# A causal attention between two expert layers: the order of work within a step

## What is computed

```python
S = where(mask, q @ k.T, 0)                # q, k with rotary positions
wk = exp(sk); zk = cumsum(wk, axis=time)   # sk, sv: clipped slot logits
p = softmax((S @ wk) * scale / zk)
wv = exp(sv); zv = cumsum(wv, axis=time)
A = where(mask, (p / zv) @ wv.T, 0)
o = A @ v
o = o * rsqrt(mean(o * o) + EPS) * gnorm_w * g * sigmoid(g)
x = x + o @ Wo
```

## Time and profile before

| | us |
|---|---|
| median of 3 runs | 529.92 (529.62 to 530.06) |
| the profiled execution | 530.72 |
| its span, first to last instruction | 528.8 |
| attention, from the first `project` to the last `add_y` | 193.5 to 368.0 |

### The profile page before, as it was taken

How to read it: one execution, slowest core, us unless ns; L and a number is a source line. 1 busy time by engine, 2 the same in 40 slices (tenths; PEclk the granted TensorE clock), 3 DMA queues, 4 the chain that set the end, 5 groups by cost and what they waited for, 6 DMA issues and landing times.

```text
span 528.8 us, 12332 instructions
## 1 busy us (share of the span) xinstructions
PE 467.3 (88%) x3895; PEld 318.7 (60%) x3895; DVE 427.0 (81%) x1139; ACT 309.1 (58%) x667; POOL 173.3 (33%) x198
## 2 busy tenths in 40 slices
PE   1788999999999568998898999885889999999996
PEld 0344566666665556676776776764455666666664
DVE  3598999999999835777778777866599999999997
ACT  3543555555555675877777777653555555555553
POOL 2999960000000364566566666534000000000000
PEclk9998999999999785999999999996599999999999
DMA  6212000000000000000000000000000000000002
GB/s 204 90 61 78 1 0 0 0 0 0 0 1 1 1 1 0 2 1 2 0 0 0 0 0 0 0 1 0 2 1 2 0 0 0 0 0 0 0 0 79
DMA packets 6697, 6.98 MB, mean 13 GB/s; under 512 B 818, under 2 KB 5170, under 8 KB 6676
## 3 DMA queue, kind: packets, MB, share of 16 engines
q1 hardware_dynamic: 6532, 6.33, 3.9%
q10 hardware_dynamic: 144, 0.39, 0.2%
HBM read 5.67 MB, written 1.05 MB: 13 GB/s over the span
## 4 chain that ended last, share of the span: by engine, by line
PE 60%; DVE 19%; issue 9%; ACT 7%; POOL 2%; DVEq 1%; DMA 1%; POOLq 0%; ACTq 0%
PE bank L1128 15%; PE bank L1140 10%; PE bank L1141 10%; PE bank L1142 10%; DVE h L804 4%; PE bank L1311 3%; DVE h_lo L810 2%; ACT gate_s L313 2%; PE bank L1325 2%; PE bank L1275 2%; DVE stats L702 2%; DVE pz L934 1%; DVE x L793 1%; DVE logit_c L926 1%; PE bank L1230 1%
## 5 line engine op out<-in xcount | busy, mean ns | idle before, releaser
L318 ACT ACTIVATE h_hi<-h 128x512 f16<-128x512 f32 x144 | 90.7, 630 | 133.3 <-DVE h L804 133.3
L804 DVE SCALAR_TENSOR_TENSOR h<-bank,gate_s 128x512 f32<-128x512 f32 x144 | 99.4, 690 | 28.4 <-ACT gate_s L313 19.0
L1128 PE MATMUL bank<-w_hi,h_hi 128*128 (+1 forms) x576 | 106.4, 221 | 12.9 <-DVE h_lo L810 8.3
L1140 PE MATMUL bank<-xt_hi,w_hi 128*128 128x512 f16 x288 | 111.8, 388 | 0.0
L1141 PE MATMUL bank<-xt_hi,w_lo 128*128 128x512 f16 x288 | 111.7, 388 | 0.0
L1142 PE MATMUL bank<-xt_lo,w_hi 128*128 128x512 f16 x288 | 111.5, 387 | 0.0
L1128 PE MATMUL bank<-w_hi,h_lo 128*128 (+1 forms) x576 | 105.9, 221 | 0.0
L1128 PE MATMUL bank<-w_lo,h_hi 128*128 (+1 forms) x576 | 105.9, 221 | 0.0
L810 DVE TENSOR_TENSOR h_lo<-h,h_hi 128x512 f16<-128x512 f32 x144 | 100.6, 698 | 0.1
L793 DVE SCALAR_TENSOR_TENSOR x<-bank,wts,x 128x128 f32<-128x128 f32 x288 | 86.5, 343 | 1.6 <-PE bank L1128 1.1
L313 ACT ACTIVATE gate_s<-bank 128x512 f32<-128x512 f32 x144 | 83.5, 580 | 0.6 <-PE bank L1142 0.6
(11 more groups left out here) (159 smaller groups left out, 855.7 us busy)
## 6 DMA issues: line engine op xcount, KB each, us to landing
wf<-in_w_ffn SPq DMA_DIRECT2D x8, 384.0 KB, 3.1
x<-in_x SPq DMA_DIRECT2D x4, 256.0 KB, 4.9
out_dram<-x SPq DMA_DIRECT2D x4, 256.0 KB, 2.3
cst<-in_consts SPq DMA_DIRECT2D x1, 455.0 KB, 5.3
wf<-in_w_ffn ACTq DMA_DIRECT2D x1, 384.0 KB, 4.2
wqkvg<-in_w_qkvg SPq DMA_DIRECT2D x1, 256.0 KB
wslots<-in_w_slots SPq DMA_DIRECT2D x3, 64.0 KB
wo<-in_w_out SPq DMA_DIRECT2D x1, 64.0 KB
```

Of the source, the lines that this page charges most:

```text
L318: act.activation(h_hi[:, g, ih, :], h32[:, ih, :], ACT.Copy).then_inc(hhi_done, 1)
L804: nc.vector.scalar_tensor_tensor(h32[:, ih, :], up_ps[ih][:, :], HS / (XS * WS), gate_s[:, ih, :], ALU.mult, ALU.mult).then_inc(hmul_done, 1)
L1128: i = mm(dst, hp[:, g, ih, c * P:(c + 1) * P], wcols(wp, e, at, D), start=(k == 0), stop=(k == 3 * IH - 1))
L1140: mm(ps[:, :], wcols(w_hi, e, at, P), xt_hi[:, ts], start=True, stop=False)
```

## The change

The lists of all four engines are put in another order. The functions, the stages, the semaphores, the buffers and the count of instructions are the same.

```diff
--- before.py
+++ after.py
@@ -458,23 +458,23 @@
                 if mid:
                     sums_log(*mid)
                 if mid:
-                    copy_value_slots(*mid)
-                if mid:
                     sums_first_inverse(*mid)
+                if front:
+                    qk_high(*front)
                 if end:
                     copy_o(*end)
                 if front:
-                    qk_high(*front)
-                if front:
                     slots_high(*front)
                 if front:
                     slots_exponent(*front)
+                if mid:
+                    copy_value_slots(*mid)
                 if front:
                     copy_qk_parts(*front)
+                if mid:
+                    soft_exp(*mid)
                 if front:
                     slots_middle(*front)
-                if mid:
-                    soft_exp(*mid)
                 if last:
                     o_square(*last)
                 if front:
@@ -655,10 +655,10 @@
                     qk_low(*front)
                 if front:
                     slots_rest(*front)
-                if front:
-                    slots_low(*front)
                 if last:
                     gate_o(*last)
+                if front:
+                    slots_low(*front)
                 if last:
                     root_o(*last)
 
@@ -1000,10 +1000,10 @@
                 front, mid, last, end = stages(i, n)
                 if front:
                     rope_multiply(*front)
+                if front:
+                    clip_slots(*front)
                 if end:
                     norm_apply(*end)
-                if front:
-                    clip_slots(*front)
                 if last:
                     mask_a(*last)
                 if last:
@@ -1012,22 +1012,22 @@
                     sums_product(*mid)
                 if mid:
                     sums_inverse(*mid)
+                if mid:
+                    soft_scale(*mid)
+                if mid:
+                    soft_min(*mid)
+                if mid:
+                    soft_centre(*mid)
+                if last:
+                    norm_shares(*last)
+                if mid:
+                    prob_scale(*mid)
+                if mid:
+                    prob_total(*mid)
+                if last:
+                    norm_squares(*last)
                 if end:
                     add_y(*end)
-                if mid:
-                    soft_scale(*mid)
-                if mid:
-                    soft_min(*mid)
-                if last:
-                    norm_shares(*last)
-                if mid:
-                    soft_centre(*mid)
-                if mid:
-                    prob_scale(*mid)
-                if last:
-                    norm_squares(*last)
-                if mid:
-                    prob_total(*mid)
                 if last:
                     norm_variance(*last)
                 if mid:
@@ -1341,34 +1341,34 @@
                 front, mid, last, end = stages(i, n)
                 if front:
                     project(*front)
+                if front:
+                    slot_logits(*front)
                 if mid:
                     running_sums(*mid)
+                if last:
+                    weights_a(*last)
                 if mid:
                     turn_v(*mid)
-                if front:
-                    slot_logits(*front)
                 if end:
                     turn_o(*end)
-                if last:
-                    weights_a(*last)
                 if mid:
                     logits_of_earlier(*mid)
+                if mid:
+                    logits_of_chunk(*mid)
                 if end:
                     out_proj(*end)
-                if mid:
-                    logits_of_chunk(*mid)
                 if front:
                     turn_qk(*front)
                 if last:
                     outputs(*last)
                 if mid:
+                    add_sums(*mid)
+                if mid:
                     add_state(*mid)
                 if mid:
-                    add_sums(*mid)
+                    turn_p(*mid)
                 if front:
                     scores(*front)
-                if mid:
-                    turn_p(*mid)
 
             pe.wait_ge(consts_loaded, 16)
             turn(0, 0)
```

More of the change, by code:

```diff
@@ L657, in attn_step @@
                     slots_rest(*front)
+                if last:
+                    gate_o(*last)
                 if front:
                     slots_low(*front)
-                if last:
-                    gate_o(*last)
                 if last:
@@ L1014, in attn_step @@
                     sums_inverse(*mid)
-                if end:
-                    add_y(*end)
                 if mid:
@@ L1023, in attn_step @@
                 if mid:
-                    soft_centre(*mid)
+                    prob_scale(*mid)
                 if mid:
-                    prob_scale(*mid)
+                    prob_total(*mid)
                 if last:
                     norm_squares(*last)
-                if mid:
-                    prob_total(*mid)
+                if end:
+                    add_y(*end)
                 if last:
@@ L1343, in attn_step @@
                     project(*front)
+                if front:
+                    slot_logits(*front)
                 if mid:
                     running_sums(*mid)
-                if mid:
-                    turn_v(*mid)
-                if front:
-                    slot_logits(*front)
-                if end:
-                    turn_o(*end)
                 if last:
@@ L1354, in attn_step @@
                 if mid:
+                    turn_v(*mid)
+                if end:
+                    turn_o(*end)
+                if mid:
                     logits_of_earlier(*mid)
+                if mid:
+                    logits_of_chunk(*mid)
                 if end:
                     out_proj(*end)
-                if mid:
-                    logits_of_chunk(*mid)
                 if front:
```

## The result

The changed kernel takes 510.97 us (median of 4, 508.95 to 512.33) against 529.99 before: a ratio of 0.963 (0.959 to 0.967), 19.0 us less. 514.0 was predicted with a range from 511 to 520, so the direction and the place were right, and the size lies outside the range, on the good side: by 0.03 us, less than the runs differ among themselves, but 3.0 us from the forecast itself.

What follows compares the result with a forecast made beforehand. TensorE's queue was taken as the bound, 8.75 us a step against 9.78. Gains of 12.4 + 0.8 + 2.7 = 15.9 took 530.7 to 514.8; less 0.8 for the median, 514.0 us, range 511 to 520.

Steps and rivals of the forecast that it cites:

- TensorE's queue is the floor and the two waits are the gain: Attention steps: TensorE loses 0.46 us at L1333 and 0.40 at L1299; without these waits its queue sets the step.
- The walk through the new step: One new attention step written out from its `project` at 0, with start times on each engine; next `project` at 8.60 us.
- The 0.65 to spare before `turn_p`: End of the softmax chain: L934 done at 7.4 us, `turn_p` takes it at 8.10, where 0.40 was lost before.
- Floor: 8.75 us a step.: TensorE's queue in an attention step: 8.60 us of work plus 0.15 for the loop's jump, against 9.78 before.
- 0.29 per pair, 0.15 per step: Loop's jump on TensorE at the end of every second step: L1299 to L1177 took 0.56 us with it, 0.27 without.
- TensorE's work in it is 9.46 - 0.86 = 8.60: One attention step of 9.46 us less its two waits, 0.86; this TensorE work stays 8.60 us in the new order.
- ScalarE ... Cost 0: Two ScalarE moves, `copy_value_slots` behind the exponentials and `qk_high` ahead of `copy_o`, each claimed to cost 0.
- `norm_apply` *"Cost 0": VectorE's `norm_apply` moved behind `clip_slots`, about 0.6 us later: cost 0, bounds -0.1 and +0.3 us a step.
- First and last steps: Attention's edges: 0.8 us gained in two steps before the twelve full ones, 2.7 in the last stretch (bounds 1.5 and 3.5).
- B: Rival: a thin margin, 0.25 for `slots_low` or 0.28 for `turn_o`, is missed; step 9.05 us, whole 518.5; chance 0.18.
- The 0.28 to spare for `turn_o`: `norm_apply` (L990) ends near 2.5 us into the step, its reader `turn_o` (L1333) starts at 2.81.
- C: Rival, slower: L904 loses its turn to L617 and L934 to L622 each step; step 10.4 us, whole 535; chance 0.04.

Runs made afterwards that it cites:

- The two loop experiments: Kernel before with four steps in the loop's body, not two: 530.02 us, ratio 1.000; changed kernel with `turn_p` behind `scores`: 510.53 us, ratio 0.963.
- each undoing: Changed kernel with `copy_o` ahead of `qk_high` again: 519.62 us, ratio 0.981; with `copy_value_slots` ahead of the first inverse again: 524.94 us, ratio 0.991.
- the three mixed kernels: Kernel before with the new list on TensorE alone: 550.17 us; on VectorE alone: 555.74 us; on TensorE and VectorE together: 546.19 us.

## Why the prediction was right, and where it failed

- *TensorE's queue is the floor and the two waits are the gain.* Right. The waits are gone and TensorE is busy throughout. Two of the twelve steps of the kernel before were long for another reason (10.28 and 10.24, L904's lost turn, at 1.64 and 1.70), which the mean of 9.78 holds; in the changed kernel L904 took 0.93 at most.
- *The walk through the new step.* Right to about 0.1 to 0.3 us at each point: L904 forecast at 4.0 and seen at 4.14, L926 5.66 and 5.96, L969 6.74 and 6.75, L934 6.95 and 6.96, `slots_low` done 8.85 and 8.81. The 0.65 to spare before `turn_p` was 0.65.
- *"Floor: 8.75 us a step."* **This step failed**, by 0.28 a step, 3.3 us over the twelve, where the whole time was missed by 3.0. It is two terms.
  - *"0.29 per pair, 0.15 per step"* for the loop's jump. I kept it as work. The two loop experiments show that it came with a wait: at the jump L1177 follows 0.23 behind the group before it, as without a jump, when that group has not waited. It should have been 0.
  - *"TensorE's work in it is 9.46 - 0.86 = 8.60"*, called the same in any order. It is 8.42 where nothing is late. The missing 0.05 up to the mean of 8.47 is L1333's late load in every second step and the 8.70 of the first step, where L1259 waited for `slots_low`. So the two terms were 0.15 and 0.18 too long, and 0.05 of waiting was left out. What differs is how far a weight load lies beside the pass before it, and the order decides which pass that is. Loads of the changed kernel:

```profile
271.89 0.52 PEld L1311 LDWEIGHTS bank<-p_t,vslot_t 64*128 64x128 f32 x4 [0.42 <-issue]
...
273.63 0.30 PEld L1268 LDWEIGHTS bank<-state,q_t 128*128 128x128 f32 x2
...
277.59 0.41 PEld L1288 LDWEIGHTS bank<-slots,qk 128*128 128x128 f32 x2
```

  Loads of the kernel before:

```profile
273.03 0.30 PEld L1268 LDWEIGHTS bank<-state,q_t 128*128 128x128 f32 x2
...
276.47 0.30 PEld L1288 LDWEIGHTS bank<-slots,qk 128*128 128x128 f32 x2
```

  L1288's load starts 0.21 before its matmul now, behind the long passes of L1282, and started 0.03 before it (276.50); L1268's starts 0.10 before it now, and started with it (273.03), behind L1311. L1288 holds 0.43 in place of 0.52, L1268 0.44 in place of 0.54, and L1333 0.16 in place of 0.26, since L1311 no longer follows it. Against that, L1259, which now has L1311 behind it, holds 0.74 (271.15 to 271.89) where I had 0.65, L1250 0.28 where I had 0.21, and L1338 0.27 where it was 0.22 (273.57 to 273.79). L1299 holds 0.23 in place of 0.27. Together that makes the 8.48 of this step out of the 8.60; the next step has 0.05 less, at L1333. That it is the order and not the two waits read too long shows with TensorE's list alone: there the queue waits about 1.5 us a step, and L1268, L1288 and L1259 hold 0.43, 0.43 and 0.74 all the same (step from 232.10). Only L1288's part was also undone by itself, in the run with `add_state` first. The Trainium skill ("TensorE: Matmul & The Clock Gate", the table at its head) says that the queue can pull a weight load ahead of matmuls in flight; the trace agrees, with L1288's 0.21. The same page of the Trainium skill (Part 3, The mechanism) says in one place that a load lies beside a running matmul only where the two use different groups of rows, and in another that a background buffer for weights allows it too; here the measurement decides against the "only", since L1288 and L1282 both use all 128 rows. L1311, whose operands have 64 rows where the others have 128, is the exception in the full steps of every one of these traces: its first load starts with its first matmul (0.00 to 0.03 before it), and so does the load of the group behind it (273.03 above).
- *"ScalarE ... Cost 0"*, twice, and `norm_apply` *"Cost 0"*. In the sum these were right, since all four lists changed; `norm_apply` cost about 0.03 a step, inside its bounds. As statements of what each move is worth they were wrong for ScalarE: each undoing costs 0.8 to 0.9 a step (9.28 and 9.39 against 8.47). The reader of L406 had three us; but the *writer*, `turn_v`, had moved back, and an instruction too early in a queue holds all that stands behind it. I had looked at who waits for the copy and not at what the copy waits for.
- *First and last steps*, 0.8 and 2.7 against 1.7 and 3.4, of which 1.0 was lost again ahead of the attention, where nothing was changed and where the traces differ by up to 2.3. That the error of the whole time (3.0) is so near that of the twelve steps (3.3) is in part luck: the edges gave 1.6 more than forecast, and the stretch ahead took 1.0 back.
- *Rivals.* B happened in small. The 0.28 to spare for `turn_o` was 0.06 in every second step, its matmul came in time but not its weight load, and it cost 0.05 to 0.06 there, about 0.03 a step where B had 0.3. `slots_low` was late for L1259 in three of the twelve steps, 0.8 us in all. C did not happen in this kernel, and its mechanism is real: with TensorE's and VectorE's lists alone, L926 and L934 lost their turns in a kernel slower than before, though that was the smaller part of its loss.

What stays open is what makes the clock fall in the three mixed kernels, and so how much of their whole time is its doing.

## What to carry to other kernels

In strictly ordered queues an order of work is one thing across all engines: three mixtures of an old and a new list were 3 to 5% slower than the old kernel, and the whole was 3.7% faster. When a step is moved, ask of every instruction on the other engines not only whether its reader still gets it in time, but whether its writer has moved behind it. And when the floor of the bound engine is worked out from a trace in which it waits, take the loop's jump behind a wait for a part of the wait, and expect the holds of the groups to change, here by 0.04 to 0.15 us each, with what stands around them.

## What the runs showed that I had not expected

- A loop's jump put 0.29 to 0.36 us between groups on TensorE when the transpose right before it had waited, 0.19 when a group of four passes stood between the two, and nothing when no wait came before it.
- Groups of matmuls of the same shapes held the queue 0.43 or 0.52, 0.44 or 0.54, by what stood before them.
- The order between VectorE and GpSimd is settled by 0.03 to 0.05 us: L990 behind L634 by 0.03 took 0.58, ahead of it by 0.05 it took 0.27, in turn from step to step.
- In all three mixtures the clock fell in the middle of the attention: with VectorE's list alone the mean granted clock was 0.57 over 15 us, where the kernel before held 1.00 throughout. Longer waits alone do not explain it: with the same waits of 1.1 to 1.4 us the same kernel held 1.00 from 280 to 340.
